# A recommendation tower on one core: a fourth gather buffer, gathers paced 1.2 pairs ahead, whole layer parts between Gram pieces

## What is computed

```python
e = stack([tbl_k[ids[:, k]] for k in range(26)], axis=1)          # 2048 x 26 x 128
combined = concatenate([dense[:, None, :], e], axis=1)            # 2048 x 27 x 128
dots = einsum('bfd,bgd->bfg', combined, combined)[:, triu_i, triu_j]   # 351 pairs a sample
h = concatenate([dense, dots, dense], axis=1)                     # 2048 x 607
h = relu(h @ W_top1 + b_top1)                                     # 512
h = relu(h @ W_top2 + b_top2)                                     # 256
y = h @ W_top3                                                    # 1
```

## Time and profile before

| | us |
|---|---|
| median of three runs | 398.69 |
| the profiled execution, its own time | 400.2 |
| its span, first to last instruction | 398.3 |
| outside the span | 1.9 |
| mean granted clock of TensorE, share of full | 0.983 |

### The profile page before, as it was taken

The page is one execution under the profiler, slowest core; times in us unless marked ns, Lnnn a source line. Parts: engine busy times, 40 slices in busy tenths (PEclk is TensorE's granted clock), DMA queues, the critical chain, the costliest instruction groups (busy, mean ns, idle before and its releaser), DMA issues.

```text
span 398.3 us, 13947 instructions
## 1 busy us (share of the span) xinstructions
PE 364.5 (92%) x6192; PEld 309.7 (78%) x6192; DVE 261.1 (66%) x748; ACT 137.0 (34%) x195; POOL 247.2 (62%) x260
## 2 busy tenths in 40 slices
PE   0857758999999999999999999999999999999798
PEld 0757747987689977997789876997789877997575
DVE  2999864990699409990599519990699419980310
ACT  3545130343325234323433334323433334324222
POOL 6777777777677665776677666775677666720000
PEclk9998996999999999999999999999999999999989
DMA  7953442223112311323122311313121312200000
GB/s 242 411 195 110 149 144 57 54 55 120 49 42 55 113 43 44 82 53 115 43 55 55 114 49 44 81 54 109 48 51 53 116 47 51 54 22 2 5 2 0
DMA packets 13677, 31.72 MB, mean 80 GB/s; under 512 B 5301, under 2 KB 6205, under 8 KB 13618
## 3 DMA queue, kind: packets, MB, share of 16 engines
q0 software_dynamic: 8192, 16.79, 15.9%
q1 hardware_dynamic: 5426, 14.04, 9.7%
HBM read 30.81 MB, written 0.01 MB: 77 GB/s over the span
## 4 chain that ended last, share of the span: by engine, by line
PE 48%; DVE 44%; issue 4%; DMA 3%; ACT 1%; SPq 0%
DVE marks L580 37%; PE flip_ps L364 12%; PE mlp_ps L412 11%; PE gram_ps L386 9%; PE flip_ps L346 6%; PE mlp_ps L421 5%; PE mlp_ps L415 3%; DVE dots L558 3%; DVE lo L588 3%; DMA feats<-small_rows 1%; DMA id_cols<-ids_in_pairs 1%; DVE pair_dots L566 1%; PE mlp_ps L430 1%; PE pairs_ps L397 1%; ACT feats L622 0%
## 5 line engine op out<-in xcount | busy, mean ns | idle before, releaser
L328 POOL DMA_INDIRECT emb<-tbl,idx x256 | 247.0, 965 | 103.8 <-issue 55.8
L580 DVE TENSOR_SCALAR marks<-id_cols,row_no 125x256 fp32r<-125x256 int16 x688 | 211.5, 384 | 4.9 <-DMA id_cols<-ids_in_pairs 4.9
L364 PE MATMUL flip_ps<-marks,hi 125*128 125x256 f32 x688 | 172.2, 291 | 18.4 <-DVE marks L580 18.0
L364 PE MATMUL flip_ps<-marks,lo 125*128 125x256 f32 x688 | 167.9, 284 | 0.0
L364 PEld LDWEIGHTS flip_ps<-marks,hi 125*128 125x128 f32 x688 | 132.6, 193 | 26.0 <-issue 21.3
L364 PEld LDWEIGHTS flip_ps<-marks,lo 125*128 125x128 f32 x688 | 132.7, 193 | 0.0
L558 DVE STREAM_TRANSPOSE dots<-gram_ps 128x864 f32<-128x864 f32 (+1 forms) x32 | 25.2, 824 | 105.8 <-PE gram_ps L386 105.8
L622 ACT COPY feats<-flip_ps 128x512 f32<-128x512 f32 x40 | 46.7, 1167 | 124.4 <-PE flip_ps L364 119.4
L386 PEld LDWEIGHTS gram_ps<-feats 128*27 128x27 f32 x4096 | 43.0, 106 | 44.4 <-issue 43.3
L544 ACT COPY feats<-flip_ps 128x512 f32<-128x512 f32 x64 | 45.0, 725 | 64.9 <-PE flip_ps L346 62.8
L386 PE MATMUL gram_ps<-feats 128*27 128x27 f32 x4096 | 54.9, 192 | 10.2 <-issue 6.8
(11 more groups left out here) (23 smaller groups left out, 63.6 us busy)
## 6 DMA issues: line engine op xcount, KB each, us to landing
id_cols<-ids_in_pairs SPq DMA_DIRECT2D x7, 640.0 KB
emb<-tbl,idx POOLq DMA_INDIRECT x256, 2.5
feats<-small_rows SPq DMA_DIRECT2D x5, 512.0 KB, 7.5
dense_sb<-dense_columns SPq DMA_DIRECT2D x4, 256.0 KB, 9.2
w1p_sb<-w_pairs SPq DMA_DIRECT2D x1, 702.0 KB
hT<-small_rows SPq DMA_DIRECT2D x1, 640.0 KB, 12.6
w1p_sb<-small_rows SPq DMA_DIRECT2D x1, 640.0 KB, 14.5
dots<-small_rows SPq DMA_DIRECT2D x1, 640.0 KB, 4.0
```

The costliest lines, as they stand in the source:

```text
L328: nc.gpsimd.indirect_dma_start(emb[:, v, (f - 1) * P:f * P], None, tables[order[f - 1]][:, :], bass.IndirectOffsetOnAxis(ap=idx[:, t, orde ...
L364: last = nc.tensor.matmul(flip_ps[:, m % FLIP_BANKS, 2 * (s % 2):2 * (s % 2) + 2, :], part[s][0:R[s], half * x + c, :], marks[0:R[s], MARK ...
L580: last = nc.vector.tensor_scalar(marks[0:R[s], MARKS_AT[h] + c, :], id_cols[0:R[s], s, :], row_no[0:R[s], s, half * x + c:half * x + c + 1 ...
```

## The change

`emb` gets a fourth slot, the pace lets the gathers run 1.2 pairs ahead rather than 0.7, and the area in SBUF where the descriptors of the gathers are written is set to 2048 bytes a partition. PE no longer cuts the layer parts: in the even stretch parts 1, 2 and 3 stand whole behind even pieces 1, 3 and 5; part 4 stands whole ahead of the odd pieces (in the last pair, too), part 5 behind odd piece 3, the third layer ahead of odd piece 7. The next tile's flips stand behind odd pieces 0, 1, 4 and 5 and no longer 0, 2, 4 and 6. ACT's list and the list of the pace follow.

```diff
-SLOTS = 3
+SLOTS = 4
-PACE_LEAD = 0.7
+PACE_LEAD = 1.2
...
             places = [looks(h) for h in range(HALVES)] + part_of_layers(0)
-            places += [piece(even, 0)] + flips(odd, 0) + [piece(even, 1), piece(even, 2)] + flips(odd, 1)
-            places += part_of_layers(1) + [piece(even, 3), piece(even, 4)] + flips(odd, 2) + [piece(even, 5)]
-            places += part_of_layers(2) + [piece(even, 6)] + flips(odd, 3) + [piece(even, 7)] + part_of_layers(3)
-            places += [piece(odd, 0)] + flips(following, 0) + [piece(odd, 1)] + part_of_layers(4)
-            places += [piece(odd, 2)] + flips(following, 1) + [piece(odd, 3), piece(odd, 4)] + flips(following, 2)
-            places += part_of_layers(5) + [piece(odd, 5), piece(odd, 6)] + flips(following, 3)
-            return places + [piece(odd, 7)] + part_of_layers(6)
+            for k in range(GROUPS):
+                places += [piece(even, 2 * k)] + flips(odd, k) + [piece(even, 2 * k + 1)] + part_of_layers(k + 1)
+            places += [piece(odd, 0)] + flips(following, 0) + [piece(odd, 1)] + flips(following, 1)
+            places += [piece(odd, 2), piece(odd, 3)] + part_of_layers(H1C + 1) + [piece(odd, 4)]
+            places += flips(following, 2) + [piece(odd, 5)] + flips(following, 3) + [piece(odd, 6)]
+            return places + part_of_layers(H1C + H2C) + [piece(odd, 7)]
...
                 layer(i - 1, 0)
-                gram(2 * i, 0)
-                flip(2 * i + 1, 0)
-                layer(i - 1, 1, range(0, 1))
-                gram(2 * i, 1)
-                layer(i - 1, 1, range(1, 3))
-                gram(2 * i, 2)
-                flip(2 * i + 1, 1)
-                layer(i - 1, 1, range(3, 4))
-                gram(2 * i, 3)
-                layer(i - 1, 2, range(0, 2))
-                gram(2 * i, 4)
-                flip(2 * i + 1, 2)
-                layer(i - 1, 2, range(2, 3))
-                gram(2 * i, 5)
-                layer(i - 1, 2, range(3, 4))
-                layer(i - 1, 3, range(0, 1))
-                gram(2 * i, 6)
-                flip(2 * i + 1, 3)
-                layer(i - 1, 3, range(1, 2))
-                gram(2 * i, 7)
-                layer(i - 1, 3, range(2, 4))
+                for k in range(GROUPS):
+                    gram(2 * i, 2 * k)
+                    flip(2 * i + 1, k)
+                    gram(2 * i, 2 * k + 1)
+                    if k + 1 < H1C:
+                        layer(i - 1, k + 1)
...
-                layer(i - 1, 4, range(0, 2))
+                layer(i - 1, H1C)
                 gram(2 * i + 1, 0)
                 next_flip(0)
-                layer(i - 1, 4, range(2, 3))
                 gram(2 * i + 1, 1)
+                next_flip(1)
+                gram(2 * i + 1, 2)
                 pair_rows(2 * i)
-                layer(i - 1, 4, range(3, 4))
-                gram(2 * i + 1, 2)
-                next_flip(1)
-                layer(i - 1, 5, range(0, 1))
                 gram(2 * i + 1, 3)
-                layer(i - 1, 5, range(1, 3))
+                layer(i - 1, H1C + 1)
                 gram(2 * i + 1, 4)
                 next_flip(2)
-                layer(i - 1, 5, range(3, 4))
                 gram(2 * i + 1, 5)
-                third_layer(i - 1, range(0, 1))
+                next_flip(3)
                 gram(2 * i + 1, 6)
-                next_flip(3)
+                third_layer(i - 1)
                 gram(2 * i + 1, 7)
-                third_layer(i - 1, range(1, 2))
...
+            layer(last - 1, H1C)
             for part in range(PIECES):
                 gram(tiles - 1, part)
                 if part == 3:
                     pair_rows(tiles - 2)
-            layer(last - 1, 4)
-            layer(last - 1, 5)
+            layer(last - 1, H1C + 1)
             pair_rows(tiles - 1)
...
-                activate(i - 1, range(0, 1))
-                keep_all(2 * i + 1, range(0, 2))
-                activate(i - 1, range(1, 2))
-                keep_all(2 * i + 1, range(2, 3))
-                activate(i - 1, range(2, 3))
-                keep_all(2 * i + 1, range(3, GROUPS))
-                activate(i - 1, range(3, H1C))
+                for k in range(GROUPS):
+                    activate(i - 1, range(k, k + 1))
+                    keep_all(2 * i + 1, range(k, k + 1))
+                activate(i - 1, range(H1C, H1C + 1))
                 if i + 1 < pairs:
                     if i + 1 >= EARLY:
-                        keep_all(2 * i + 2, range(0, 1))
+                        keep_all(2 * i + 2, range(0, 2))
                     keep_pairs(2 * i)
-                    activate(i - 1, range(H1C, H1C + 1))
-                    if i + 1 >= EARLY:
-                        keep_all(2 * i + 2, range(1, 3))
                     activate(i - 1, range(H1C + 1, H1C + H2C))
                     if i + 1 >= EARLY:
-                        keep_all(2 * i + 2, range(3, GROUPS))
+                        keep_all(2 * i + 2, range(2, GROUPS))
                     keep_y(i - 1)
             keep_pairs(tiles - 2)
-            activate(pairs - 2, range(H1C, H1C + H2C))
+            activate(pairs - 2, range(H1C + 1, H1C + H2C))
...
-    nc = bacc.Bacc("TRN2", target_bir_lowering=False, num_devices=1)
+    nc = bacc.Bacc("TRN2", target_bir_lowering=False, num_devices=1, dynamic_dma_scratch_size=2048)
```

More of the change, by code:

```diff
@@ L82, in tower @@
     AHEAD = max(h for h in range(1, HALVES + 1) if sum(SIZES[:h]) <= MARK_CHUNKS)
-    assert CHUNKS == 3 and H1C == 4 and H2C == 2 and GROUPS == 4
+    assert H1C == GROUPS == 4 and H2C == 2 and PIECES == 2 * GROUPS
     ctx = ExitStack()
@@ L399, in pair_rows, with layer @@
                 last.then_inc(s_pairs, 1)
-            def layer(i, q, parts=range(4)):
+            def layer(i, q):
                 bank = mlp_ps[:, q % 2, 0:2 * P]
-                if q == 0 and 0 in parts:
+                if q == 0:
                     pe.wait_ge(s_xT, 2 * i + 2)
-                if q != 1 and (i or q) and 0 in parts:
+                if q != 1 and (i or q):
                     pe.wait_ge(s_act, STEPS * i + max(q - 1, 0))
[L410 to L417, removed]
+                if q < H1C:
+                    for c in range(CHUNKS):
+                        nc.tensor.matmul(bank, w1p_sb[0:CHUNK, c, q * P:(q + 1) * P],
+                                         xT[0:CHUNK, c, :, :], start=(c == 0), stop=False)
+                    last = nc.tensor.matmul(bank, w1d_sb[:, q * P:(q + 1) * P],
+                                            dense_sb[:, i % DENSE_PAIRS, :], start=False, stop=True)
+                else:
+                    for c in range(H1C):
                         if q == H1C:
@@ L422, in layer, with third_layer @@
                                                 h1T[:, c, :], start=(c == 0), stop=(c == H1C - 1))
[L423 to L427, removed]
+                last.then_inc(s_mm, 1)
+            def third_layer(i):
+                for c in range(H2C):
                     pe.wait_ge(s_act, STEPS * i + H1C + c + 1)
@@ L431, in third_layer @@
                                             start=(c == 0), stop=(c == H2C - 1))
-                if H2C - 1 in parts:
-                    last.then_inc(s_mm, 1)
+                last.then_inc(s_mm, 1)
             def looking_up(i, groups=range(LOOK_GROUPS)):
```

## The result

403.18 us, median of four runs (403.07 to 404.12), against 398.81 for the kernel before in the same comparison: ratio 1.0116, 95% interval 1.0098 to 1.0134. The kernel is 4.4 us slower; the forecast was +2.3.

The account below looks back on a forecast made before the run. TensorE (43.83 us a turn) and a loop through VectorE (44.5) both set the pace. Terms -0.3 + 0.6 + 2.6 + 0.3 - 0.9 = +2.3 us, from the median 398.69 to 401.0; range 397.5 to 404.0.

Parts of the forecast that it names:

- end term: End of the last pair: even piece 7's +0.87 less a gain of 1.8, together -0.9 us.
- even piece 7's 0.87: Even stretch: four more layer instructions ahead of even piece 7, at 0.217 each, make it 0.87 us later.
- turn 1 to 2: Pair 1: four gaps fewer among the odd pieces, partly offset by stalls at issue and later marks; -0.3 us.
- turn 2 to 3: Pair 2: odd transposes had waited 0.24 us for PE, so only 0.63 of 0.87 arrives; +0.6 us.
- turns 3 to 6, three: Turns bound by VectorE grow from 44.5 to 45.4 us; +2.6 us, and +0.3 for gathers.
- turn 6 to 7: Turn to pair 7: TensorE is the bound with its 43.83 us as before; 0.
- the layers' terms: Terms of the new layer order: pair 1 -0.3, pair 2 +0.6, three turns +2.6, end -0.9 us.
- the gathers' term: VectorE's stretch: freely running GpSimd fits 24.8 gathers rather than 24, 0.15 us a turn for two turns; +0.3 us.
- The loop through VectorE: Even piece 7, VectorE's work, look-ups and even pieces: 31.0 us on VectorE and 13.5 on TensorE, 44.5 a turn.
- Gain 5.2 - 3.4 = 1.8: Last pair's end, part 4 moved ahead of the odd pieces: 1.8 us gained if stall and low clock come again.
- The room of the odd side: Odd piece 7 10.3 us after even piece 7, VectorE needing 10.7: it never waits there, so odd-side gains buy nothing.
- The small area and the fourth slot: Gathers: the fourth slot opens nothing; the smaller descriptor area taken as 0, its holding GpSimd a rival at 5%.

Follow-up runs that it names:

- r1: The kernel before, unchanged, run again for a second trace: median 398.42 us, ratio 1.0000.
- r4: The kernel before with only layer part 4 moved ahead of the odd pieces in the last pair: 398.06 us, ratio 0.9988.
- r3: The kernel before with only the new order of layers on PE and ACT; three slots, pace 0.7, default area: ratio 1.0077, +2.9 us.
- r16: The kernel before without the gathers of tiles 8 to 15, on the slow chip only: 446.6 us against 501.5, ratio 0.886.
- r17: The kernel before with the third layer's last two instructions ahead of odd piece 7 instead of behind it: ratio 1.0067, +2.3 us.
- r7: The kernel before with the fourth slot and the 2 KB area, pace 0.7 kept, on the slow chip only: ratio 1.013 (0.990 to 1.036).
- r2: The kernel before with the fourth slot, pace of 1.2 pairs and 2 KB area, layers in the old order: ratio 1.0040, +1.6 us.
- r10: The kernel before with only the pace lead set to 1.2 pairs, on a usual chip: ratio 1.0030, +0.8 us by medians.
- r6: The kernel before with only the pace lead set to 1.2 pairs, on the slow chip: median 523.0 us against 501.0 to 501.5.
- r18: The kernel before with part 3 wholly behind even piece 7 and the third layer wholly behind odd piece 7: ratio 1.0023.

## Why the forecast fell short

Direction and mechanism were right, the size was half. The step that failed is the carrying over to the median: "on the median 398.69 the same terms give 401.0", with an end term priced at a low clock that only the traced execution had. Against that execution (398.3) the changed kernel's 401.1 is +2.8, close to +2.3, and that is in part luck: from pair 7's even transposes to the end that execution took 27.65 us and the changed kernel 25.05, a gain of 2.60 and not 1.8. Set against the second trace of the kernel before, with the even transposes of pair 1 to 7 as marks (the forecast counted its turns between layer parts 0, so that even piece 7's 0.87, which it adds at the end, stands here in the first row):

| stretch | forecast | measured |
|---|---|---|
| to pair 1 | +0.87 | 104.48 - 103.88 = +0.60 |
| turn 1 to 2 | -0.3 | +0.04 |
| turn 2 to 3 | +0.63 | 45.54 - 44.57 = +0.97 |
| turns 3 to 6, three | +2.61, and +0.3 for gathers | +1.15, +0.94, +0.87 |
| turn 6 to 7 | 0 | +0.27 |
| behind pair 7's even piece | -1.8 | 25.05 - 25.39 = -0.34 |
| sum | +2.3 | +4.5 |

The first two rows carry little: in the three traces that have the old order there (before, r1, r4) the stretch to pair 1 took 103.17, 103.88 and 103.38 us and turn 1 to 2 took 45.53, 45.62 and 44.82. Turns 2 to 6 agree within 0.1 us. By halves, the layers' terms came to +2.0 and the layers alone cost +2.9; the gathers' term was +0.3 and they alone cost +1.6.

- **The loop through VectorE.** Right: idle 13.5 to 14.27 and 14.53 (forecast 14.4), none ahead of the odd transposes, bound turns 45.4 to 45.7 (forecast 45.4), last turn 43.85, and the layers alone lengthen the wait by 0.82 against 0.87. That the three turns came to the forecast +2.9 is partly two errors that cancel: the layers alone made them 0.65 longer, not 0.87, and the gathers added more than 0.15.
- **The term that was mis-sized** is "Gain 5.2 - 3.4 = 1.8 ... as long as stall and low clock come again". They didn't. No run shows the 3.4, an estimate of 0.43 us for each of eight layer instructions at a granted clock of 0.51: the eight took 1.99 us at 1.00 in the changed kernel, and 1.99 in r3 and r4. At that clock the sixteen instructions take 3.55 us to the next start, eight and the wait 2.56, a gain of 1.0, and the stall at issue was 1.78 us against 1.26, which takes back half. Behind pair 7's piece 0.34 was gained instead of 1.8. The forecast had noted that its trace was 1.5 us above the median, and did not ask where those 1.5 lay; they lay in the very row that it subtracted from. This is 1.5 of the 2.2 missing; with the gathers' 1.3 more that is over 2.2, and the layers' shorter turns pay some of it back.
- **The gathers** were forecast at +0.3 and alone cost +1.6 by medians. The price of one, 0.19, was right (0.18 with the bare marks of r16), and so was the end of the flow, 332.79 for 330. Wrong were the size and the length: 24.8 gathers in VectorE's stretch "rather than 24", 0.15 us a turn, "for two turns". Freely running GpSimd cost 0.3 to 0.5 in each of three turns. In pair 4 of the kernel before 23 gathers start in VectorE's stretch (GpSimd busy for 22.2 us from 237.84 to 268.82), and with the pace alone 25 (23.8 us from 238.61 to 270.11): two more where the forecast had 0.8, and at 0.18 each 0.36 us. The old pace held GpSimd back there (it stood 1.05 and 0.88 us ahead of 240.32 and 242.20). Of the 0.3 to 0.5 a turn 0.29 lay in the 28 marks, and the rest in the wait for the even piece (+0.16) with three edits, and in the 58 marks (18.2 us) with the pace alone. Why the wait moved is open.
- **The room of the odd side.** "Which is 0.6 behind the start of even piece 7": the lag of 0.6 us from a piece's start to VectorE's was counted for the even piece and not for the odd one. With it 10.75 + 0.6 stands against 10.7 + 0.6, no room. It did not change this sum, as the changed kernel's odd piece came earlier, but it hid that the kernel before was balanced on two loops, and r17 shows what that costs.
- **Pair 1.** The four gaps went, and a stall of 1.30 us at issue came (109.99). The row shows +0.04 for -0.3, inside the bounds named and inside that turn's own scatter; the layers alone show 45.28 - 45.62 = -0.34.
- **The small area and the fourth slot.** No gather of the changed kernel took over 1.56 us and no flip waited for one; the pace alone carries the cost of a turn. How many gathers the area holds no run shows; the direct test, r7, was lost to the slow chip.

## What to carry to other kernels

Look for every loop that closes, not for the first: where an engine never idles ahead of one of its waits, compute that wait's room with the same lag as for the other, for a zero there means that a second loop is tight. If the profiled execution is off the median, find the row in which the difference lies before a term is taken from that row. And work that fills a gap belongs behind the last thing that the other engine waits for, as long as it still fits under that engine's stretch.

## What the runs showed that I had not expected

A gather that is issued while VectorE's marks run back to back can be shut out until they end. It was 6.47 us above; in r17, pair 1:

```profile
106.38 7.43 DVE L580 TENSOR_SCALAR marks<-id_cols,row_no 125x256 fp32r<-125x256 int16 x28
107.59 6.34 POOL L328 DMA_INDIRECT emb<-tbl,idx  x1 [0.98 <-PE gram_ps L386]
```

and in the trace that the forecast rests on, pair 1 as well:

```profile
110.64 2.90 POOL L328 DMA_INDIRECT emb<-tbl,idx  x1 [1.79 <-PE gram_ps L386]
```

All three end 0.1 us behind the last mark, and all were released by a pace wait inside the marks. In the three traces of the usual chips with a lead of 1.2 pairs (the changed kernel, r2 and r10), where GpSimd ran without a pause from 90 to 240 us, none took over 1.57 us. The longer lead is no cure, though: on the slow chip r6, the pace alone, had three gathers of 10.6 us. In r17 and r18 the block lasted about 24 marks (6.34 and 6.47 us, at 0.266 a mark), and yet most gathers beside marks were not blocked at all: of r17's 256 no other took over 1.56 us. Which gathers are shut out, and by what, no run shows. So the longer lead cost 0.3 to 0.5 us in each of three turns, and no run shows that it bought anything: in the kernel before no flip waited for a gather.
